# Pairs of blocks in a six-layer local-attention stack: one feed-forward and root chain for 256 tokens, attend with a feature-major result

## The reference

```
for each of 6 layers:
    shift: features 64..127 of a token are those of the token before it
    qkv = shifted @ Wqkv                      # 16 heads of 64
    q, k = l2norm(q) * qs, l2norm(k) * ks     # per head
    q, k = rotary(q), rotary(k)               # cos and sin tables with a scale
    attention in windows of 32: each window sees itself and the one before
    x = x + attention @ Wo
    shift again; layer norm; W1 (2 x 341) -> a * gelu(gate) -> W2
    x = x + the feed-forward
```

## Time and profile before

| what | value |
|---|---|
| median of 3 runs | 1886.72 us (1884.89 to 1888.19) |
| profiled execution | 1885.08 us, span 1882.9 us |
| granted TensorE clock, mean | 0.968 of 2.4 GHz |
| PE busy | 1716.6 us (91%) |
| DVE busy | 1664.4 us (88%) |
| ACT busy | 1363.7 us (72%) |
| POOL busy | 1289.6 us (68%) |

### The profile page before, as it was taken

How to read it: one execution, slowest core, us unless ns; L and a number is a source line. 1 busy time by engine, 2 the same in 40 slices (tenths; PEclk the granted TensorE clock), 3 DMA queues, 4 the chain that set the end, 5 groups by cost and what they waited for, 6 DMA issues and landing times. The chain is left out here.

```text
span 1882.9 us, 83647 instructions
## 1 busy us (share of the span) xinstructions
PE 1716.6 (91%) x33456; PEld 1329.2 (71%) x33456; DVE 1664.4 (88%) x3697; ACT 1363.7 (72%) x2647; POOL 1289.6 (68%) x724
## 2 busy tenths in 40 slices
PE   3947899999999999999999999999999999999984
PEld 2524677777777777777777777777777777777773
DVE  5788889999999999899999899999899999999975
ACT  3334678777777877877777787787777778778762
POOL 1538767777767777777777677777677777777741
PEclk8878999999999999999999999999999999999996
DMA  3001222222322222322212322222321222222220
GB/s 133 1 1 46 81 69 58 53 67 78 91 65 67 54 58 78 102 54 67 67 48 75 111 53 59 67 60 62 111 65 49 64 67 68 66 67 59 53 68 23
DMA packets 80680, 121.62 MB, mean 65 GB/s; under 512 B 16776, under 2 KB 29574, under 8 KB 79750
## 3 DMA queue, kind: packets, MB, share of 16 engines
q1 hardware_dynamic: 80646, 121.14, 24.1%
HBM read 19.36 MB, written 1.05 MB: 11 GB/s over the span
## 5 line engine op out<-in xcount | busy, mean ns | idle before, releaser
L1174 POOL TENSOR_TENSOR rot<-rot,root 128x1024 f32<-128x1024 f32 x192 | 365.3, 1903 | 392.3 <-DVE root L1048 392.3
L716 PE MATMUL r<-wqkv,xs 128*128 (+1 forms) x1152 | 528.6, 595 | 5.3 <-ACT xs L879 3.9
L1159 POOL TENSOR_TENSOR rot<-rot,rot_sin 128x1024 f32<-128x1024 f32 x192 | 451.2, 2373 | 0.0
L902 ACT ACTIVATE squares<-r 128x512 f32<-128x512 f32 x384 | 229.0, 597 | 298.1 <-PE r L716 295.2
L716 PEld LDWEIGHTS r<-wqkv,xs 128*128 128x128 f32 x1152 | 205.0, 191 | 194.6 <-issue 187.2
L1010 DVE TENSOR_TENSOR rot_sin<-r,table 128x512 f32<-128x512 f32 x384 | 245.3, 679 | 0.0
L1005 DVE TENSOR_TENSOR rot<-r,table 128x1024 f32<-128x1024 f32 x192 | 234.0, 1219 | 12.5 <-ACT squares L902 8.4
L1166 POOL TENSOR_TENSOR squares<-squares 128x512 f32<-128x512 f32 x192 | 241.6, 1281 | 0.6 <-ACT squares L902 0.4
L721 PE MATMUL r<-square,rot 128*128 128x128 f32 x1536 | 206.0, 279 | 36.1 <-DVE rot_sin L1010 30.4
L1179 POOL TENSOR_TENSOR sm<-sm,rowmax 128x1024 f32<-128x1024 f32 x96 | 182.6, 1902 | 65.7 <-DVE rowmax L1058 65.7
L721 PEld LDWEIGHTS r<-square,rot 128*128 128x128 f32 x1536 | 172.0, 143 | 58.5 <-DVE rot_sin L1010 50.8
(11 more groups left out here) (131 smaller groups left out, 3165.1 us busy)
## 6 DMA issues: line engine op xcount, KB each, us to landing
vwin<-vtok SPq DMA_DIRECT2D x576, 128.0 KB
vwin<-vtok SPq DMA_DIRECT2D x384, 64.0 KB
wqkv<-in_wqkv SPq DMA_DIRECT2D x6, 1536.0 KB, 6.3
wo<-in_wo SPq DMA_DIRECT2D x6, 512.0 KB, 3.9
w<-in_w SPq DMA_DIRECT2D x6, 341.0 KB, 3.0
x<-in_x SPq DMA_DIRECT2D x4, 256.0 KB, 3.7
rope<-in_rope SPq DMA_DIRECT2D x1, 1024.0 KB
out_x<-y SPq DMA_DIRECT2D x4, 256.0 KB, 2.3
```

The lines of the kernel that those rows point to most:

```text
L716: pe.matmul(dst[:, c * 512:(c + 1) * 512], xs1[:, u, 0:P], w.rearrange("p a n -> p (a n)"), start=True, stop=True).then_inc(S[done], 1)
L902: last = act.activation(squares[:, k, c * 512:(c + 1) * 512], src[:, c * 512:(c + 1) * 512], ACT.Square)
L1159: pool.tensor_tensor(r, r, rot_sin[:, k, :, :, :].rearrange("p h a d -> p h (a d)"), ALU.add)\
L1174: pool.tensor_tensor(r, r, bcast(root[:, k * HEADS:(k + 1) * HEADS], 2, DH), ALU.mult)\
```

## The change

Every engine's step now covers a pair of blocks, m = 0 to 47, with two or four lags between stages. The feed-forward chain (out-projection, centering, variance, up, down) runs once for 256 columns. The roots of four sets of heads and two rows of the norm are found in one chain of 66 columns. The up-projection goes in three pieces, each with its own place. mid holds the state after the first residual. xT and mid carry one column of zeros ahead of each sequence, so that the shift is a read one column to the left, and the carry copies leave.

GpSimd divides the probabilities by their sums before the transpose (weigh). Attend takes the values as the stationary operand, 64 columns wide, and moves 32 columns of probabilities; its result is feature-major, so normalise and the transposes of the attention output leave. vwin, sm, probs, pT, qT have two places. spread_v(n) waits for attended, which starts at 2, so it waits for attend(n-2); copy_v(n) still waits for the spread of n-1.

```diff
             def spread_v(n, u):
...
                 sp.wait_ge(S["v_copied"], turn)
-                sp.wait_ge(S["vwin_free"], turn)
+                sp.wait_ge(S["attended"], turn)
...
-                    sp.dma_start(vwin[at:at + WIN, 0, :, :], heads_of(vtok[P - WIN:P, 1 - u, e, :, :]))\
+                    sp.dma_start(vwin[at:at + WIN, u, 0, :, :], heads_of(vtok[P - WIN:P, 1 - u, e, :, :]))\
...
-            def attend(n, dst):
+            def attend(n, u, dst):
...
                 for i in range(FT // 2):
-                    for s in range(2):
-                        for e in range(2):
-                            half = slice(2 * WIN * e, 2 * WIN * (e + 1))
-                            at = 512 * e + DH * (2 * i + s)
-                            for w in range(NW):
+                    for w in range(NW):
+                        for s in range(2):
+                            for e in range(2):
+                                half = slice(2 * WIN * e, 2 * WIN * (e + 1))
                                 rows = slice(WIN * w, WIN * (w + 1))
-                                last = pe.matmul(dst[rows, at:at + DH], pT[half, (FT // 2) * s + i, rows],
-                                                 vwin[half, w, 2 * i + s, :], start=True, stop=True)
-                last.then_inc(S["vwin_free"], 1)
+                                at = 512 * e + P * i
+                                last = pe.matmul(dst[DH * s:DH * (s + 1), at + WIN * w:at + WIN * (w + 1)],
+                                                 vwin[half, u, w, 2 * i + s, :],
+                                                 pT[half, u, (FT // 2) * s + i, rows], start=True, stop=True)
+                last.then_inc(S["attended"], 1)
...
+            def weigh(n, u):
+                pool.wait_ge(S["inverted"], n + 1)
+                pool.tensor_tensor(probs[:, u, :, :], probs[:, u, :, :], bcast(rinv[:, u, :], 2, 2 * WIN), ALU.mult)\
+                    .then_inc(S["weighted"], 1)
```

More of the change, by code:

```diff
@@ L634, in layers, with runs, first, pair_at @@
         block = ctx.enter_context(nc.Block())
[L636 to L644, removed]
-        def run(eng, step):
[L648 to L657, removed]
+        LAG, FILLED, BEHIND = 2, 6, 4
+        def runs(m):
+            return not isinstance(m, int) or 0 <= m < PAIRS
+        def first(n):
+            return isinstance(n, int) and n == 0
+        def run(eng, step):
+            for m in range(FILLED):
+                step(m)
+            with eng.Fori(FILLED, PAIRS) as m:
+                step(m)
+            for m in range(PAIRS, PAIRS + BEHIND):
+                step(m)
+        def pair_at(m):
+            return (m % PPL) * W2 + (m % PPL) // PPB
         @block.sync
@@ L681, in _ @@
             sp.wait_ge(S["cleared_pool"], 1)
-            for n in range(4):
+            for n in range(6):
                 spread_v(n, n % 2)
@@ L727, in score @@
                 pe.wait_ge(S["kT_copied"], n + 1)
-                if not (isinstance(n, int) and n == 0):
+                if not first(n):
                     pe.wait_ge(S["k_carried"], n)
@@ L779, in spread_rstd, with ff_var @@
-            def spread_rstd(n):
-                pe.wait_ge(S["refined"], ROOT_OPS * (n + 4))
-                if runs(n - 1):
-                    pe.wait_ge(S["x_ready"], NB + n)
-                pe.matmul(pm[:, 0:P], root[:, 2 * HEADS:ROOTS].broadcast_to([P, P]), ident,
-                          start=True, stop=True).then_inc(S["rstd_spread"], 1)
-            def ff_up(n, dst):
-                pe.wait_ge(S["xn2_ready"], n + 1)
-                pe.wait_ge(S["w1_loaded"], 16 * (n // NB + 1))
+            def ff_var(m):
+                pe.wait_ge(S["xc_squared"], m + 1)
+                for u in range(2):
+                    last = pe.matmul(pm_norm[:, u:u + 1], xcsq[:, u * P:(u + 1) * P], mean_w[:, 0:1],
+                                     start=True, stop=True)
+                last.then_inc(S["var_done"], 1)
@@ new lines, in spread_rstd, with ff_up @@
+            def spread_rstd(m):
+                pe.wait_ge(S["refined"], ROOT_OPS * (m + LAG + 1))
+                for u in range(2):
+                    last = pe.matmul(pm_norm[:, u * P:(u + 1) * P],
+                                     root[:, QK_ROOTS + u:QK_ROOTS + u + 1].broadcast_to([P, P]), ident,
+                                     start=True, stop=True)
+                last.then_inc(S["rstd_spread"], 1)
+            def ff_up(m, t, dst):
+                if t == 0:
+                    pe.wait_ge(S["xn2_ready"], m + 1)
+                    pe.wait_ge(S["w1_loaded"], 16 * (m // PPL + 1))
+                at, rows = FFT[t]
@@ L790, in ff_up @@
                 for half in range(2):
-                    for t, (at, rows) in enumerate(FFT):
-                        last = pe.matmul(dst[0:rows, 512 * half + t * P:512 * half + (t + 1) * P],
-                                         w1[:, half * FF + at:half * FF + at + rows], xn2[:, :],
-                                         start=True, stop=True)
+                    last = pe.matmul(dst[0:rows, half * W2:(half + 1) * W2],
+                                     w1[:, half * FF + at:half * FF + at + rows], xn2[:, :], start=True, stop=True)
@@ L1215, in _ @@
                 for n in range(q * PB, (q + 1) * PB):
[L1216 removed]
+                    at = columns(n)
+                    last = pe.transpose(ps[:, n * P:(n + 1) * P], xT[:, at:at + P], ident)
                 last.then_inc(turned, 1)
```

708 lines of the change are left out of this document (406 added, 302 removed).

## The result

The changed kernel takes 2088.8 us (median, 2086.32 to 2090.17), the one before 1887.45 us in the same series: a ratio of 1.107, 95% interval 1.105 to 1.109. It is slower, by the mechanism of the forecast, but by 139 us more than the forecast's 1950, and outside its range. The profiled span is 2084.4 us, the mean clock 0.919 where it was 0.968.

A forecast was written before the change was run, and what follows sets the result against it. TensorE and VectorE were taken to pace each other before; after, the ring at 35.2 us a pair plus 1.4 of clock loss gives T = 36.6, and 265 + 46 T gives 1949, so 1950 us, range 1840 to 2020.

The forecast's parts named there:

- the ring: Odd block's value copy waits for the spread, that for the step's last attend, TensorE for the copy: 35.2 us a pair.
- The new idle piece: TensorE idle ahead of a transpose that waits for the value copy, 4.0 us in one piece in every pair.
- the ring's sum: 9.2 us from attend's end through the value copy plus 26.0 of TensorE groups in order: 35.2 us a pair.
- TensorE's 26.0: TensorE's groups in order from the transposes behind the value copy to the end of the next even block's attend.
- the 9.2: From attend's slot end: spread issue and landing 8.0 us, semaphore 0.1, value copy 1.07.
- attend's bounds: Attend's slot on TensorE, taken as 1.9 us between 1.42 and 2.84; the period then 34.2 to 37.1 us.
- The clock: TensorE's clock drops to half around the idle piece: 1.4 us lost a pair, bounds 0 and 1.7.
- ring at full clock: Rival, chance 0.20: the same waits set the pace without clock loss, 35.2 us a pair, 1884 us.
- Fill and tail: Start and end of the layers: first attend 47 us after the start, last two blocks 35, tail 24; off by 10.
- The rival with the dearer ring: Chance 0.06: attend at 2.84 us because fewer moving columns save no time, clock low, 38.5 us a pair, 2036 us.
- the first rival: Chance 0.16: TensorE's own work sets the pace, no wait through the spread, 31.2 us a pair, 1700 us.

The follow-up runs named there:

- e1: Changed kernel with four places instead of two for the copied values (vtok), so the value copy waits for older spreads: 1808.26 us, ratio 0.959 to the kernel before.
- e7: Changed kernel whose spreads each issue two more DMAs of 32 KB to a tile nobody reads: 2158.48 us.
- e4: Changed kernel with the even block's attend ahead of the down projection in TensorE's list instead of behind it: 2020.77 us.
- e8: e1 with two more DMAs of 32 KB in each spread, to a tile nobody reads: 1809.78 us.
- e2: Changed kernel with the odd block's value projection made three times, 3.4 us of extra matmuls in each pair: 2024.15 us.
- e3: Changed kernel with the load of the next layer's QKV weights issued two spreads later: 2068.20 us.
- e9: e1 with attend's matmuls given 16 moving columns instead of 32, leaving out half of attend's output: 1810.87 us.

## Why the prediction was wrong in size and right in kind

**The mechanism: right, and shown.** The copy waits for the spread, the spread for the last attend of the step, and TensorE for the copy, once in every pair. Breaking the ring takes 280 us away (e1), lengthening it by 1.27 us adds 70 (e7), shortening it by 1.4 makes plain pairs 2.1 us shorter (e4), and the DMAs that count on it are free beside it (e8). The new idle piece was predicted at 4.0 us and is 3.55.

**The step that failed: the ring's sum, "26.0. The period is 35.2 us for a pair".** At full clock the ring measures 36.95 (e2), 1.75 more: TensorE's 26.0 are 27.4, and the 9.2 from attend's end to the transposes are 9.5. That is 46 x 1.75 = 80 of the 139 us. By its own terms:
- odd attend to even attend: 19.35 predicted, 20.38 measured. The slots of up and down, 0.86 and 1.29 in the sum, are 1.40 and 1.49: 0.37 of it is a wait for VectorE's minus_half, the rest that each record of 256 columns takes 0.25 us there and not 0.215. Center is 0.54 for 0.43, variance 0.36 for 0.22, Q and K 3.54 for 3.44, Q 1.81 for 1.72, attend 2.0 for 1.9; the transposes and the score are 0.02 to 0.13 shorter.
- even attend to odd attend: 15.8 predicted, 16.55 in e2. The copy starts 8.36 us after attend's end, not 8.1; the up piece of 85 rows takes 1.05 for 0.86, spreading the roots 0.64 for 0.47, attend 2.0 for 1.9.

None of these is large. The range held only attend's bounds and those of the clock; that some twenty estimated slots could come out too small in the sum was in no bound. As each 0.1 us counts 46 times, 1.75 us weighed more than either.

**The clock: right on average, at its upper bound, and that in part by luck.** 1.4 us was taken of 0 to 1.7; it is 38.62 - 36.95 = 1.7 (46 x 0.27 = 12 us in all). The argument was right for two pairs of three, with low parts of 3.5 and 3.2 us and a loss of 1.1 and 1.4; in the first of them some of the low part does lie in the gap. In every third pair the low part is 6.8 us and the loss 2.5, above the bound. The Trainium skill (TensorE: Matmul & The Clock Gate, Part 1) says that idling brings the engine back to the low clock; the trace agrees, with a granted clock of 0.54 behind 3.55 us without a matmul. The rival "ring at full clock" fell with it.

**A term that was missing: the layer starts.** The prediction looked at the weight loads nowhere. At four layer starts a pair takes 5.3 us more, 21 us in the sum; e3 shows that it is the QKV load ahead of the spread. Before, the spread had 3.9 us to spare, and the spacings behind this load are at most 0.04 us longer. What one block a layer lost there (18.5 us between attends after 17.3 to 17.4) was TensorE's wait for another load, the second feed-forward weights:

```profile
507.20 0.94 PE L803 MATMUL pm<-hid,w 128*128 128x128 f32 x6 [1.69 <-DMA w<-in_w]
```

So the QKV load became a price when the spread came onto the ring.

**Fill and tail.** The first attend ends at 189.3, predicted 188.4: 1 us. The first five pairs take 203 us, where the prediction had 5 x 36.6 - 4 = 179, so they are longer than full pairs and not shorter; 10 of the 24 us are the ring's and the clock's terms above, 14 are new, and their cause stays open. The last pair takes 36.5 for 35. From the end of block 94's attend to the last write of xT 31.5 us pass, not 24. In all 80 + 12 + 21 for the pairs, 14 for the first five, and 1 + 1.5 + 7.5 for the rest make 137 of the 139 us.

**Attend.** 1.9 was taken between 1.42 and 2.84; it is 2.0. The Trainium skill (TensorEngine Tiling, Performance Considerations) says that a matmul with one moving column takes as long as one with 60, and e9 agrees: 32 or 16 columns, 1.98 to 2.0 us. The upper bound that was drawn from the rule, 2.84, was not reached. The rival with the dearer ring (2036) so failed in its reason, though its number came closer.

**The engines that were to stay beside it.** GpSimd's 29.8 us a pair: 29.7 measured in the pair that starts at 941.30. VectorE's 28: 28.75 there. TensorE alone, 31.2, was the first rival's pace: e1 measures 32.9, and 1808 us where that rival had 1700. Its short groups were underpriced by the same 1.7 us, 79 of the 108; the rest lies in the first five pairs and the tail.

## What to carry to other kernels

When a change widens a step or moves a group to its end, follow each buffer's reuse round once (who waits for whose release, through the DMA queue too) and ask whether the round closes within one step. If it does, every delay on it counts in full, among them clock loss and a weight load in the same queue. Two more places in one buffer turned a loss of 11% into a gain of 4%. An experiment that adds useless work in the suspected idle time and one that adds the same work without the ring tell a ring from a busy engine at once, by their sign. And where a period is the sum of twenty slots that recur 46 times, the range needs a term for the sum of their errors.

## What had not been expected of the hardware

- More matmuls made the kernel faster: 3.4 us more in each pair, 65 us less in all, because a gap of 3.55 us on TensorE halves the clock of the work behind it (0.54 and 0.61 in the two windows of 2 us).
- The same gap doesn't always cost the same. Behind gaps of 3.55 to 3.61 us the low part was 3.2, 3.5 or 6.8 us long in three pairs in a row; and of the 36 plain pairs of e4, with gaps of about 2.6 us, 25 show a mean clock of 0.90 or 0.91 from even to odd attend and 11 show 1.00.
- A matmul on a tile of 64x64 with 32 or with 16 moving columns takes the same 15.5 ns of the engine's time (128 in 1.98 us), one of 64x32 with 32 columns 9.7 ns (128 in 1.24 us); that of before, 64x32 with 64 columns, took 11 ns. On attend's slot the trade of fewer moving columns for wider stationary tiles lost 0.6 us (1.42 to 2.0).
- With a spread of ten DMAs the value copy starts 8.4 us after the attend that the spread waits for, and 13.9 us after it when a load of 1.5 MB is issued 0.7 us ahead of the spread.
